# Third norm of a two-layer decoder taken into the loop of its self-attention, and the bias of the values moved behind the softmax

## What is computed

```python
x = x + _L0_xattn_ref(_layernorm(x), ctx_1024, ...)          # 16 heads of 64, 361 keys
x = x + _L0_ffn_ref(_layernorm(x), ...)                      # block-quantised product
x = x + _L1_attn_ref(_layernorm(x), W_attn, b_attn, W_proj, b_proj, rel_emb)
x = x + _L1_xattn_ref(_layernorm(x), ctx_1024, ctx_1024, Wq, Wk, Wv, mask)
x = x + _L1_ffn_ref(_layernorm(x), w_gate, w_up, w_down)

def _L1_attn_ref(x, ...):                                    # 16 heads of 16, causal
    q, k, v = split(x @ W_attn.T + b_attn)
    att = softmax(where(causal, q k^T / 4 + rel_bias, -inf))
    return (att v) @ W_proj.T + b_proj
```

## Time and profile before

| what | value |
| --- | --- |
| median of 3 runs | 1466.62 us (1465.25 to 1466.91) |
| the profiled execution, own time | 1470.03 us |
| its span, first to last instruction | 1468.2 us |
| PE, DVE, ACT, POOL busy | 1277.8, 1043.7, 737.6, 256.4 us |
| granted TensorE clock, mean | 0.942 |
| chain that ended last, PE / DVE | 51% / 16% of the span |

### The profile page before, as it was taken

The page is one execution under the profiler, slowest core; times in us unless marked ns, Lnnn a source line. Parts: engine busy times, 40 slices in busy tenths (PEclk is TensorE's granted clock), DMA queues, the critical chain, the costliest instruction groups (busy, mean ns, idle before and its releaser), DMA issues.

```text
span 1468.2 us, 27745 instructions
## 1 busy us (share of the span) xinstructions
PE 1277.8 (87%) x9826; PEld 1087.1 (74%) x9826; DVE 1043.7 (71%) x2592; ACT 737.6 (50%) x1808; POOL 256.4 (17%) x314
## 2 busy tenths in 40 slices
PE   4889888797899999999999999999879978969319
PEld 4878788796777777877778787877667756759318
DVE  5866466745567777777777777777589967885974
ACT  4442423325465555555655555565446643436473
POOL 3325252525100000000000000000044421000100
PEclk9899999998999999999999999999799989989759
DMA  9000101022100000000000000000020022300001
GB/s 282 31 22 1 44 1 44 1 77 80 35 11 11 12 1 11 10 11 10 11 11 10 1 10 11 10 1 1 1 58 2 3 66 62 100 7 1 0 0 46
DMA packets 34547, 40.66 MB, mean 28 GB/s; under 512 B 4889, under 2 KB 29066, under 8 KB 34442
## 3 DMA queue, kind: packets, MB, share of 16 engines
q1 hardware_dynamic: 33614, 39.24, 8.8%
q10 hardware_dynamic: 828, 0.14, 0.1%
HBM read 35.36 MB, written 4.01 MB: 27 GB/s over the span
## 4 chain that ended last, share of the span: by engine, by line
PE 51%; DVE 16%; issue 5%; ACT 4%; POOL 1%; DVEq 0%; ACTq 0%; POOLq 0%
PE bank L764 8%; PE bank L766 7%; PE bank L765 7%; PE bank L975 4%; PE bank L959 4%; PE bank L967 3%; PE bank L935 3%; ACT prob L1634 2%; DVE amax L2454 2%; DVE nmx L2270 2%; PE bank L1208 1%; PE bank L1226 1%; DVE kTl L2048 1%; PE bank L996 1%; PE bank L1293 1%
## 5 line engine op out<-in xcount | busy, mean ns | idle before, releaser
L1634 ACT ACTIVATE prob<-bank,nmx 100x361 f32<-100x361 f32 x256 | 142.7, 560 | 156.6 <-DVE nmx L2270 155.7
L2270 DVE TENSOR_REDUCE nmx<-bank 100x1 f32<-100x361 f32 x256 | 124.2, 526 | 22.8 <-PE bank L959 15.7
L690 POOL TENSOR_TENSOR frstd<-fmoments,eps 100x1 f32<-100x1 f32 x32 | 6.2, 193 | 648.5 <-DVE fmoments L2213 648.4
L764 PE MATMUL bank<-cxTh,wxkh 128*128 128x362 f32 x256 | 99.9, 390 | 2.8 <-DVE kTl L2048 2.8
L975 PEld LDWEIGHTS bank<-pT,vv 128*64 128x64 f32 (+1 forms) x1536 | 71.2, 139 | 37.5 <-issue 28.2
L975 PE MATMUL bank<-pT,vv 128*64 128x100 f32 (+1 forms) x1536 | 96.6, 261 | 1.9 <-DVE oTl L2047 1.8
L2287 DVE TENSOR_SCALAR prob<-prob,rsum 100x361 f32<-100x361 f32 x256 | 92.9, 405 | 4.5
L967 PE MATMUL bank<-ident,prob 100*128 100x100 f32 (+1 forms) x768 | 90.7, 254 | 1.5 <-DVE prob L2287 1.5
L967 PEld LDWEIGHTS bank<-ident,prob 100*128 100x128 f32 (+1 forms) x768 | 85.5, 153 | 7.1 <-DVE prob L2287 2.6
L2047 DVE TENSOR_TENSOR oTl<-bank,oTh 128x100 fp32r<-128x100 f32 x128 | 32.9, 257 | 81.2 <-ACT oTh L1620 78.0
L1620 ACT CAST oTh<-bank 128x100 fp32r<-128x100 f32 x128 | 31.8, 249 | 112.6 <-PE bank L975 112.4
(11 more groups left out here) (403 smaller groups left out, 3794.8 us busy)
## 6 DMA issues: line engine op xcount, KB each, us to landing
cx<-in_ctx_dram SPq DMA_DIRECT2D x32, 128.0 KB, 2.1
xc<-in_ctx_dram SPq DMA_DIRECT2D x32, 128.0 KB
parked_weights<-parking SPq DMA_DIRECT2D x9, 256.0 KB, 5.6
mask_i<-in_mask_BxS_ik_dram SPq DMA_DIRECT2D x16, 141.0 KB
w<-in_L_attn_W_dram SPq DMA_DIRECT2D x2, 1024.0 KB, 13.6
cx<-in_ctx_dram SPq DMA_DIRECT2D x16, 105.0 KB, 2.1
xc<-in_ctx_dram SPq DMA_DIRECT2D x16, 105.0 KB
x<-in_x_dram SPq DMA_DIRECT2D x4, 400.0 KB
```

The source lines that it names most:

```text
L764: pe.matmul(o, wh, mh, start=start, stop=False)
L1634: nc.scalar.activation(prob[:, h % 4, :], bank[S_BANKS[e]][0:T, 0:S], ACT.Exp, bias=nmx[:, h:h + 1], accum_out=psum_[:, h:h + 1]).then_inc ...
L2270: nc.vector.tensor_reduce(nmx[:, h:h + 1], bank[S_BANKS[e]][0:T, 0:S], AX_X, ALU.max, negate=True).then_inc(xa_max, 1)
```

## The change

Four things are changed together.

1. The bias of the values is no longer added. In pair 4 of the first batch of the first cross-attention PE multiplies it with `wproj`, and DVE adds the result to `bproj`; POOL lays the bias out as `fqT` before.
2. `values_out` on DVE (an addition) becomes `values_copied` on ACT (a copy), ahead of the batch's four copies `p1T`.
3. The norm of a batch runs in the attention's loop: `row_moments_3` on DVE, `rstd_of` on POOL, `row_normalised_3` on DVE an iteration later in the middle of `scores_out`, `row_transposes_3` on PE behind `heads_weighted` of the batch after that, in bank 4, and `rows_copied_3` on ACT. The last three batches are transposed in the first three slots of the second cross-attention.
4. `norm(2)`, `all_transposes(2)` and `all_copies(2)` are gone. SP loads the parked weights only when the last transposes are done, since they lie over `z_row` and `fb`.

```diff
             sp.dma_start(bproj[:], a["L1_attn_b_proj"].partition_broadcast(T)).then_inc(relb_in, 16)
-            sp.dma_start(bv1[:], a["L1_attn_b_attn"][2 * D:3 * D].partition_broadcast(T)).then_inc(relb_in, 16)
             with sp.Fori(2, B) as b:
...
             sp.wait_ge(a1_x, B)
+            sp.wait_ge(ff_t, 3 * B)
             sp.wait_ge(park_out, 16 * 9)
...
+            value_bias = COL["L1_attn_b_attn"] + 2 * KD
+            nc.gpsimd.tensor_copy(fqT[:], vec[:, value_bias:value_bias + KD].unsqueeze(2).broadcast_to([P, KD, T])).then_inc(xa_bv, 1)
             def rstd_of(event, part):
...
                 pool.wait_ge(ff_q, 2 * j + 2)
+                pool.wait_ge(a1_sb, 5)
                 nc.gpsimd.tensor_tensor(x[:, j, :], x[:, j, :], bproj[:], ALU.add).then_inc(a1_rows, 1)
...
                     row_with_bias(B - 1)
+                if b > 1:
+                    rstd_of(2 * B + b - 1, 1)
+            rstd_of(3 * B - 1, 1)
+            rstd_of(3 * B, 1)
...
-            def both_transposes(src):
+            def both_transposes(src, o):
                 for k in range(KD):
-                    mm = pe.transpose(bank[W_BANK][:, k * T:(k + 1) * T], src[:, k * P:(k + 1) * P], ident[0:T, 0:T])
+                    mm = pe.transpose(bank[o][:, k * T:(k + 1) * T], src[:, k * P:(k + 1) * P], ident[0:T, 0:T])
                 mm.then_inc(ff_t, 1)
...
                 pe.wait_ge(ff_q, 2 * j + 2)
-                both_transposes(z_row)
+                both_transposes(z_row, W_BANK)
+            def row_transposes_3(b, o):
+                pe.wait_ge(ff_q, 2 * B + b + 1)
+                both_transposes((z_row, fb)[b % 2], o)
...
                     mirrored(p)
+                if starts and not odd and p == 4:
+                    pe.wait_ge(a1_sb, 4)
+                    pe.wait_ge(xa_bv, 4)
+                    for k in range(KD):
+                        mm = pe.matmul(bank[W_BANK][0:T, 0:D], fqT[:, k, :], wproj[:, k, :], start=(k == 0), stop=(k == KD - 1))
+                    mm.then_inc(a1_rb, 1)
                 if p == 2 and not (starts and not odd):
...
                     if k == 0 and starts and not odd:
-                        pe.wait_ge(a1_sb, 4)
+                        pe.wait_ge(a1_sb, 5)
                     if k == 0 and not starts:
...
                     pe.wait_ge(a1_ca, 4 * b - 1)
+                    if b > 3:
+                        pe.wait_ge(ff_c, 2 * B + b - 3)
                 for h in range(4):
...
                 heads_weighted(b)
+                if b > 2:
+                    row_transposes_3(b - 3, TB[0])
                 if b + 2 < B:
...
             heads_output(B - 1)
-            pe.wait_ge(a1_x, B)
-            all_transposes(2)
...
                 if there and r == 0:
+                    pe.wait_ge(ff_c, 2 * B + G * g + G)
                     for m in range(KD):
...
                     pe.wait_ge(x1_uc, c + 1)
-                    if not (isinstance(g, int) and g == 0):
+                    if isinstance(g, int) and g == 0:
+                        pe.wait_ge(ff_c, 3 * B)
+                    else:
                         pe.wait_ge(x1_x, c)
...
                     mm.then_inc(x1_u, 1)
+                if isinstance(g, int) and g == 0 and r < 3:
+                    if r:
+                        pe.wait_ge(a1_x, B)
+                        pe.wait_ge(ff_c, 3 * B - 3 + r)
+                    row_transposes_3(B - 3 + r, (Y_BANK, QK_BANK, QK_BANK)[r])
...
+            def rows_copied_3(b, o):
+                act.wait_ge(ff_t, 2 * B + b + 1)
+                nc.scalar.copy(zT[:, b // 2, :, T * (b % 2):T * (b % 2 + 1)], bank[o][:, 0:KD * T].rearrange("d (k q) -> d k q", k=KD)).then_inc(ff_c, 1)
             def mirror_copied(j):
...
+            def values_copied(b):
+                act.wait_ge(a1_vm, b + 1)
+                if b == 0:
+                    act.wait_ge(a1_ones, 1)
+                if b > 1:
+                    act.wait_ge(a1_av, b - 1)
+                for e in range(2):
+                    heads = bank[TB[1]][0:T, 0:D].rearrange("k (n e d) -> k n e d", e=2, d=DH1)[:, :, e, :]
+                    ins = nc.scalar.copy(v1z[:, b % 2, :, e, DH1 * e:DH1 * (e + 1)], heads)
+                ins.then_inc(a1_v, 1)
             def head_exponents(b):
...
             queries_out(0)
+            values_copied(0)
             rows_copied(B - 2, zT[:, PAIRS - 1, :, 0:T])
...
             for b in range(B):
+                if b + 1 < B:
+                    values_copied(b + 1)
                 heads_copied(b, 0)
...
                     head_exponents(b + 1)
-            all_copies(2, TURN[2])
+                if b > 2:
+                    rows_copied_3(b - 3, TB[0])
...
                     nc.scalar.copy(uxT[:, o], bank[6][:, 0:KD * T].rearrange("p (k q) -> p k q", k=KD)).then_inc(x1_uc, 1)
+                if isinstance(g, int) and g == 0 and r < 3:
+                    rows_copied_3(B - 3 + r, (Y_BANK, QK_BANK, QK_BANK)[r])
...
-            all_deviations(TURN[3])
+            all_deviations(TURN[2])
             def rows_high(g):
                 for k in range(KD):
-                    act.wait_ge(ln_t, 2 * KD * NG + KD * g + k + 1)
+                    act.wait_ge(ln_t, KD * NG + KD * g + k + 1)
                     nc.scalar.copy(zTh[:, k, N * g:N * (g + 1)], bank[Z_BANKS[g] + k][:, 0:N]).then_inc(f1_zh, 1)
...
                 final = ends and odd
+                if starts and not odd and p == 4:
+                    dve.wait_ge(a1_rb, 5)
+                    nc.vector.tensor_tensor(bproj[:], bank[W_BANK][0:T, 0:D], bproj[:], ALU.add).then_inc(a1_sb, 1)
                 if p == 2 and not starts:
...
-            def values_out(b):
-                dve.wait_ge(a1_vm, b + 1)
-                if b == 0:
-                    dve.wait_ge(a1_ones, 1)
-                if b > 1:
-                    dve.wait_ge(a1_av, b - 1)
-                for e in range(2):
-                    heads = lambda ap: ap.rearrange("k (n e d) -> k n e d", e=2, d=DH1)[:, :, e, :]
-                    ins = nc.vector.tensor_tensor(v1z[:, b % 2, :, e, DH1 * e:DH1 * (e + 1)], heads(bank[TB[1]][0:T, 0:D]),
-                                                  heads(bv1[:]), ALU.add)
-                ins.then_inc(a1_v, 1)
             def biased(b, j):
...
                 highest(b, 1)
+                if b > 2:
+                    row_normalised_3(b - 3)
                 biased(b, 3)
...
-            def row_stats_1(b):
+            def row_moments_3(b):
                 dve.wait_ge(a1_x, b + 1)
-                return nc.vector.bn_stats(stats_all[:, b, :], x[:, b, :])
-            values_out(0)
+                link(nc.vector.bn_stats(fstats[:, 1, :], x[:, b, :]))
+                nc.vector.bn_aggr(fmoments[:, 1, :], fstats[:, 1, :]).then_inc(ff_v, 1)
+            def row_normalised_3(b):
+                dve.wait_ge(ff_r, 2 * B + b + 1)
+                dve.wait_ge(ff_t, 2 * B + max(b - 1, 0))
+                nc.vector.tensor_scalar((z_row, fb)[b % 2][:], x[:, b, :], fmoments[:, 1, 0:1], frstd[:, 1:2], ALU.subtract,
+                                        ALU.mult).then_inc(ff_q, 1)
             scores_out(0)
...
                 if b + 1 < B:
-                    values_out(b + 1)
                     scores_out(b + 1)
...
                     outputs_added(b - 1)
+                    row_normalised_3(b - 2)
                 if b:
-                    row_stats_1(b - 1)
+                    row_moments_3(b - 1)
             heads_scaled(B - 1)
+            row_normalised_3(B - 2)
             outputs_added(B - 1)
-            row_stats_1(B - 1)
-            norm(2)
+            row_moments_3(B - 1)
+            row_normalised_3(B - 1)
```

21 lines of the change are left out of this document (10 added, 11 removed).

## The result

The changed kernel takes **1473.78 us** (median of 6 runs, 1471.73 to 1476.34) where the kernel before takes 1466.59 (6 runs): a ratio of 1.0052, 95% interval 1.0039 to 1.0065. It is slower by 0.5%, outside the forecast's range. The profiled execution took 1474.24 us, its span 1472.4. Of the later executions that this text draws on, three were disturbed (one of the changed kernel at 1658.91 us, two of the kernel before at 1661.68 and 2464.21) and are left out of every ratio.

A forecast was written before the change was run, and what follows sets the result against it. PE was taken to bound the loop, DVE 0.5 us behind; the handover, PE's waits and half clock. Terms -14.2 + 3.6 + 4.0 + 1.7 + 1.3 + 0.5 + 2.2 - 0.5 = -1.4 gave 1465.2 us, range 1457.5 to 1471.5.

The forecast's parts named there:

- The folded bias: +2.2: First cross-attention, pair 4 of first batch: DVE waits for PE's bias product, so PE ends 2.2 us late, once.
- The last batches: +0.5: Last batches of second self-attention, DVE the bound: normalisation and aggregation lie between addition to `x` and reciprocal, +0.5 us.
- The loop: +3.0: Second self-attention loop: PE's added transposes cost 1.7 us, waits for ACT's copy to `zT` in five batches 1.3.
- The start: -0.5: Start of second self-attention: ACT makes the first `v1z` 4 us earlier, but DVE's saved additions set the gain, -0.5 us.
- The handover: -14.2: Second self-attention to second cross-attention: PE goes on at once, full clock returns earlier, third context's scores come 14.2 us sooner.
- The reload: +3.6: Second cross-attention: context 4's load stands behind the parked weights in SP's queue, so PE waits 3.6 us.
- the casts: +4.0: Second cross-attention: POOL's four casts fall amid slots where DVE is busy and hold its instructions, +4.0 us.
- A clock that falls again there: Sign of a wrong forecast: PE's clock falling again in the second group of slots of the second cross-attention.
- Loads and casts were not hidden: Rival, chance 0.2: in the second cross-attention loads and casts stay hidden, 3.6 and 4.0 vanish, 1457.6 us.
- The casts did not stop DVE throughout: Rival, chance 0.2: each cast holds DVE from start to end, 10.0 us instead of 4.0, giving 1471.2 us.
- The normalisation was not held by POOL in the loop: Rival, chance 0.1: POOL's subtractions hold DVE's `row_normalised_3` in the self-attention loop, +3.2 us, giving 1468.4 us.

The follow-up runs named there:

- experiment 14: Kernel before with only the table of vectors two rows longer, rows that nothing reads: 1470.87 us, ratio 1.0020.
- experiment 4: Changed kernel with the values of batches 0 and 1 copied to `v1z` by DVE, by ACT from batch 2 on: 1470.35 us, ratio 1.0016.
- experiment 3: Changed kernel with ACT's copy to `zT` between the next batch's second and third exponents, no longer behind the fourth: 1471.00 us, ratio 1.0018.
- experiment 10: Changed kernel with late bias addition, `zT` copy between exponents, first values on DVE, third row buffer, parked loads last, plus values' copy before fourth exponent: 1458.64 us.
- experiment 9: Changed kernel with POOL's four casts held back until the second cross-attention has ended, parked loads issued as before: 1473.82 us, ratio 1.0046.
- experiment 13: Version of experiment 10 with POOL's casts held back until DVE has added the last row's mask: 1460.57 us, ratio 0.9948.

## Why the forecast was wrong

*The folded bias: +2.2.* The step itself was right: B grew by 2.02, behind a wait of 4.43 us. What failed is that the term was taken to be all of the folded bias. **The two rows added to the table of vectors were given no cost and no sentence; they take 2.9 us (experiment 14)**, most of it, by the traces, between 55 and 397 us, where the forecast looked at nothing. The diff ahead of the prediction does not show that line either; it is the edit of experiment 14.

*The last batches: +0.5.* **This step failed most.** It measured 3.6 and 4.4 us. The prediction looked at DVE there, and at ACT only in the loop, where the exponents are early. In the last batches the exponents wait for POOL, so a copy queued behind the fourth is late however short it is, and PE's next transposes need its bank: a wait of 2.15 us in both traces. With that wait and the clock at 1.00 throughout, G is 20.14 (experiment 4), 1.2 us over before. The other 2.3 and 3.1 us are half clock, for which the step had no term: the granted clock over G was 0.87 and 0.79. It comes and goes. In the seven traces with the copy behind the exponents G is 20.1 to 23.3 us (mean 22.2), in the four with the copy between them 19.4 to 22.5 (mean 20.6).

*The loop: +3.0.* It measured 0.8. The wait of 0.28 us behind the copy came in every second batch, as forecast. But PE's eight transposes had 0.22 us of waiting inside their 1.11, which no idle time showed, and in the changed kernel they take 0.89, since ACT makes `v1z` early. The prediction read no idle time before them as no wait. Experiments 3 (1.21 with the values late) and 10 (0.89 with them early) show both sides.

*The start: -0.5.* The second trace has -1.1 in D and +0.2 in E, the first +0.4 and +2.3. PE has the values early and stands idle 2.71 and 2.58 us later on; how long it then keeps half clock differs between executions.

*The handover: -14.2.* Right: -14.1 in the first trace, -12.5 in the second, where the clock stayed low for longer.

*The reload: +3.6, and the casts: +4.0.* The wait measured 3.60 and 3.33. The casts are 2.6 us (experiment 9), not 4.0: the two terms were added as if they were independent, but half of the casts' 9.9 us fell on idle time of DVE (3.7 and 1.3 us) behind the very wait for context 4. Against that, PE restarts at half clock behind the wait, which had no term: 1.5 us. Together I grew by 7.9 against 7.6; that the sum fits so well is luck. A clock that falls again there was among the forecast's own signs of being wrong. DVE's ports behaved as the Trainium skill says ("SBUF — State Buffer", section "Who interferes with whom"): held were masks (2.91 us) and additions with both inputs in SBUF (1.83 us in experiment 10); the additions with an input in PSUM, statistics and reductions were not (experiment 13).

*The rivals.* Loads and casts were not hidden. The casts did not stop DVE throughout. The normalisation was not held by POOL in the loop (0.40 us each). The kernel became slower for reasons that none of them had. The profiled execution of before, from which I summed, lay 3.4 us above its median; stretch A of such an execution is as long as that of the changed kernel, which hid the first term from a comparison of two traces.

From the first reciprocal on, the stretches add up to +3.8 us in the first trace and +1.1 in the second. With the 2.9 of the rows that is +6.7 and +4.0 us, where the two series of runs have 7.6 and 4.1 by their ratios; as some of the 2.9 may lie behind the first reciprocal too, the agreement is rough. Why the two rows cost what they do stays open.

## What to carry to other kernels

A copy that frees a bank belongs where its source is ready, not behind instructions of the same engine that wait for a third one: ask of each queue what the last few iterations wait for, since their bound is another than the loop's. When a stage is made to start earlier, move what was hidden under its old gap too; here the parked loads and the casts needed a new place, and with it the same change is 9 us faster instead of 7 slower. And compare medians with one part undone, even the trifling ones: two rows of constants cost more than most of the terms that were argued over. Before a gain is read off one pair of traces, look at the granted clock of the stretch in both: of the 3.1 us that experiment 3 seemed to show, 0.75 are left when both have full clock.
